# A transformer layer with attention and mixture of experts: the prologue rebuilt, in pairs of tiles

## The reference

```
h  = layernorm(x) * (1 + ca) + sa
xn = layernorm(h) * gamma + beta
q, k, v = xn @ qkv                       (256 wide each)
a  = softmax(q k^T / 16, causal) @ v @ o_proj + h
x  = x + ga * a
h2 = layernorm(x) * (1 + cb) + sb
gate: sigmoid(h2 @ gate_w^T), 2 of 4 groups, 4 of 32 experts, weights normalised, times 2
moe(h2): each expert takes at most 64 rows: silu(h2 w1) * (h2 w3) @ w2
shared(h2): silu(h2 sg) * (h2 su) @ sd
x  = x + gb * (moe(h2) + shared(h2))
```

## Time and profile before

| what | us |
|---|---|
| median of 3 runs | 187.12 (186.43 to 188.12) |
| span of the profiled execution (the page states no other time of its own for it) | 195.2 |
| TensorE busy | 155.4 (80%) |
| VectorE busy | 106.3 (54%) |
| ScalarE busy | 63.8 (33%) |
| GpSimd busy | 72.3 (37%) |
| first product of TensorE starts | 8.49 |
| product with vo for tile 3 ends | 60.5 |
| first scatter starts | 80.52 |

### The profile page before, as it was taken

How to read it: one execution, slowest core, us unless ns; L and a number is a source line. 1 busy time by engine, 2 the same in 40 slices (tenths; PEclk the granted TensorE clock), 3 DMA queues, 4 the chain that set the end, 5 groups by cost and what they waited for, 6 DMA issues and landing times.

```text
span 195.2 us, 2961 instructions
## 1 busy us (share of the span) xinstructions
PE 155.4 (80%) x1002; PEld 109.1 (56%) x1002; DVE 106.3 (54%) x377; ACT 63.8 (33%) x168; POOL 72.3 (37%) x96
## 2 busy tenths in 40 slices
PE   0298679999989999852992149995999969979984
PEld 0164437875558758631840034584877657569763
DVE  1589947459566979982142736792444523300453
ACT  3437876421457165330000125100264435400000
POOL 8129301995000000477776058540003726560000
PEclk9999999999999999999579556999699999999999
DMA  4999999999999900021100000009401101116992
GB/s 123 301 385 393 417 420 378 350 348 349 348 348 348 299 9 0 27 95 50 32 17 11 0 3 11 9 8 291 156 0 33 49 14 54 42 65 250 399 325 104
DMA packets 24670, 33.47 MB, mean 171 GB/s; under 512 B 2817, under 2 KB 19958, under 8 KB 24656
## 3 DMA queue, kind: packets, MB, share of 16 engines
q1 hardware_dynamic: 22352, 30.86, 46.1%
q0 software_dynamic: 2304, 2.44, 3.8%
HBM read 23.45 MB, written 13.83 MB: 191 GB/s over the span
## 4 chain that ended last, share of the span: by engine, by line
PE 30%; DVE 22%; DMA 12%; issue 11%; another core or an unknown queue 10%; ACT 6%; POOL 6%; SPq 1%; POOLq 1%; DVEq 0%; ACTq 0%
PE bank L997 7%; PE bank L1282 6%; DMA w_sb<-results 5%; POOL slots L437 4%; PE bank L1301 3%; DMA w_sb<-in_L_wmod_dram 3%; PE bank L1329 3%; PE bank L1261 3%; DVE bmax L768 2%; DMA arena<-slots 2%; DVE st L679 2%; POOL results L447 2%; DVE rows L789 2%; PE bank L1101 1%
## 5 line engine op out<-in xcount | busy, mean ns | idle before, releaser
L437 POOL DMA_INDIRECT slots<-rows,slot_idx x32 | 31.5, 984 | 52.0 <-DVE slot_idx L868 41.6
L447 POOL DMA_INDIRECT results<-arena,res_idx x16 | 15.6, 975 | 29.3 <-DVE arena L953 24.4
L1127 PE MATMUL bank<-arena 128*128 128x256 f32 x72 | 19.0, 411 | 0.4 <-issue 0.4
L1282 PE MATMUL bank<-w_sb,arena 128*64 128x128 f32 x256 | 17.7, 285 | 0.0
L1282 PEld LDWEIGHTS bank<-w_sb,arena 128*64 128x64 f32 x256 | 14.9, 143 | 2.4 <-issue 1.8
L1127 PEld LDWEIGHTS bank<-arena 128*128 128x128 f32 x72 | 14.3, 206 | 3.0 <-issue 0.9
L997 PE MATMUL bank<-w_sb,h2T 128*128 128x512 f32 x12 | 7.5, 760 | 8.5 <-DMA w_sb<-in_L_wmod_dram 8.5
L966 DVE TENSOR_TENSOR h2T<-h2T,bank 128x256 f32<-128x256 f32 x8 | 3.4, 422 | 15.5 <-ACT h2T L641 15.5
L539 ACT ACTIVATE h2T<-bank,modc 128x128 f32<-128x128 f32 x16 | 6.5, 455 | 14.1 <-PE bank L1135 12.5
L520 ACT ACTIVATE prob<-bank,nmax 128x512 f32<-128x512 f32 (+3 forms) x12 | 6.9, 581 | 12.4 <-DVE nmax L772 12.4
L1245 PE MATMUL bank<-ones_bf,ident_bf 128*128 128x128 bf16 x160 | 9.8, 219 | 1.1 <-issue 1.1
(11 more groups left out here) (155 smaller groups left out, 308.9 us busy)
## 6 DMA issues: line engine op xcount, KB each, us to landing
w_sb<-in_L_ffn_w_dram SPq DMA_DIRECT2D x12, 1024.0 KB, 12.4
results<-prob SPq DMA_DIRECT2D x1, 4096.0 KB, 22.0
w_sb<-results SPq DMA_DIRECT2D x7, 512.0 KB, 7.1
slots<-prob SPq DMA_DIRECT2D x1, 2112.0 KB, 12.1
arena<-slots SPq DMA_DIRECT2D x4, 528.0 KB, 5.5
xin<-in_L_attn_x_dram SPq DMA_DIRECT2D x4, 256.0 KB, 4.6
w_sb<-in_L_wmod_dram SPq DMA_DIRECT2D x1, 1024.0 KB, 9.7
out_dram<-base SPq DMA_DIRECT2D x8, 128.0 KB, 3.5
```

Source lines behind the costliest of these rows:

```text
L437: g.indirect_dma_start(out=slots_d, out_offset=bass.IndirectOffsetOnAxis(ap=slot_idx[:, i, k:k + 1], axis=0), in_=rows[:, i, :], in_offset ...
L447: g.indirect_dma_start(out=results_d, out_offset=bass.IndirectOffsetOnAxis(ap=res_idx[:, r:r + 1], axis=0), in_=ob[:, (r // 2) % 4, (r % 2 ...
L1127: last = t.matmul(bank[6][:, 0:H], probT[:, i % 2, j, :], vo[:, j, :], start=(j == 0), stop=(j == i))
L1282: last = t.matmul(bank[4 + g % 2][CAP * side:CAP * side + CAP, o:o + F], slotT[:, k, CAP * e:CAP * e + CAP], w[:, e, k, :], start=(k == 0) ...
```

## The change

It rebuilds what comes before tile 3.

- Loads: the modulation matrix comes in three loads instead of two, the first of them ahead of everything on SP's queue; x comes by pairs between the others; c is loaded from ScalarE's queue. `prob` is zeroed last of GpSimd's constants.
- TensorE first runs 56 products of a constant with itself (`keep_warm(WARM0)`), whose result nobody reads.
- h is made on VectorE alone, by pairs: (x - mean) * (1 + ca), then * rstd + sa, both in one instruction each per tile; ScalarE's `xhat_tile` and GpSimd's part are gone.
- q is made per pair in one bank and copied out by ScalarE; ScalarE also copies out v. The gate rows ga and gb are made one by one; GpSimd starts the residual rows after the first.
- The first tiles' scores, exps and products are mixed with the later pairs' h, q and v on every engine.

```
-            for j in range(NB):
+            def load_x(j):
                 sp.dma_start(xin[:, 2 * j:2 * j + 2, :], x_d[:, 2 * j:2 * j + 2, :]).then_inc(x_loaded[j], 16)
-                if j == 1:
-                    sp.dma_start(wmod_a, wmod_d[:, :, 0:512]).then_inc(wmod_loaded[0], 16)
+            sp.dma_start(wmod_a, wmod_d[:, :, 0:512]).then_inc(wmod_loaded[0], 16)
+            load_x(0)
             sp.dma_start(qkv_sb, qkv.rearrange("(p k) n -> p k n", k=KT)).then_inc(qkv_loaded, 16)
-            sp.dma_start(wmod_b, wmod_d[:, :, 512:1536]).then_inc(wmod_loaded[1], 16)
+            load_x(1)
+            sp.dma_start(wmod_b[:, :, 0:512], wmod_d[:, :, 512:1024]).then_inc(wmod_loaded[1], 16)
...
+            load_x(2)
+            load_x(3)
+            sp.dma_start(wmod_b[:, :, 512:1024], wmod_d[:, :, 1024:1536]).then_inc(wmod_loaded[2], 16)
...
-                    sp.wait_ge(qT_mm, 2)
+                    sp.wait_ge(qT_mm, NB)
...
-            pool.wait_ge(mod01, 1)
+            pool.wait_ge(gagb_done, 1)
             for i in range(NT):
-                if i % 4 == 0:
-                    continue
-                pool.wait_ge(xhat_done, i + 1)
-                g.tensor_tensor(h[:, i, :], h[:, i, :], mod[:, 1, :], ALU.mult).then_inc(xhat_scaled, 1)
-                if i % 2:
-                    pool.wait_ge(xhat_scaled, scaled_by_pool(i))
-                    g.tensor_tensor(h[:, i, :], h[:, i, :], mod[:, 0, :], ALU.add).then_inc(h_pool, 1)
...
+                pool.wait_ge(h_done, i + 1)
                 g.tensor_tensor(base[:, i, :], h[:, i, :], mod[:, 2, :], ALU.mult).then_inc(rbase_h, 1)
...
             def make_h(j):
...
+                for i in (2 * j, 2 * j + 1):
+                    step(v.scalar_tensor_tensor(out=h[:, i, :], in0=xin[:, i, :], scalar=mv1[:, i, 0:1],
+                                                in1=mod[:, 1, :], op0=ALU.subtract, op1=ALU.mult))
+                refine(X_STAT[j])
+                settle()
+                for i in (2 * j, 2 * j + 1):
+                    v.scalar_tensor_tensor(out=h[:, i, :], in0=h[:, i, :], scalar=rstd[:, 0, i:i + 1],
+                                           in1=mod[:, 0, :], op0=ALU.mult, op1=ALU.add).then_inc(h_done, 1)
+                dve.wait_ge(h_done, 2 * j + 2)
+                moments(H_STAT[j], h)
...
+            def keep_warm(count):
+
+                for _ in range(count):
+                    t.matmul(bank[0][:, 0:P], ones_bf[:, :], ones_bf[:, :], start=True, stop=True)
...
-                if j % 2:
+                if j == 1:
                     pe.wait_ge(modc_done, 1)
```

More of the change, by code:

```diff
@@ L307, in adaln_attention_moe @@
         MOD_BANK = [bank[b] for b in (0, 2, 7)]
+        Q_BANK = [bank[b] for b in (1, 3, 1, 3)]
+        VO_BANK = [bank[b] for b in (6, 7, 7, 7)]
         block = ctx.enter_context(nc.Block())
@@ L697, in refine @@
                                              in1=seed[:, which, r], op0=ALU.add, op1=ALU.mult))
-            def x_moments(n):
-                for j in (2 * n, 2 * n + 1):
-                    dve.wait_ge(x_loaded[j], 16)
-                moments(n, xin)
             def shift(n, done):
@@ L784, in add_attention @@
                 dve.wait_ge(x2_done, i + 1)
-                moments(6 + i, base)
+                moments(X2_STAT[i], base)
             def norm_x2(i):
-                refine(6 + i)
+                refine(X2_STAT[i])
                 v.tensor_scalar(rows[:, i, 0:H].rearrange("q (k p) -> q p k", k=KT),
@@ L1060, in turn_h, with project_q @@
                 last.then_inc(ring_filled, 1)
-            def project_q(half):
-                pe.wait_ge(ring_drained, ring[f"hn{2 * half + 1}"] + 1)
+            def project_q(j):
+                pe.wait_ge(ring_drained, ring[f"hn{j}"] + 1)
                 pe.wait_ge(wqk_done, 1)
-                if half:
-                    pe.wait_ge(qT_act, 1)
-                    pe.wait_ge(qT_dve, 1)
+                if j >= 2:
+                    pe.wait_ge(qT_done, j - 1)
                 for d in range(KT):
-                    last = product(bank[1 + 2 * d][:, :], [(wqk[:, k, P * d:P * d + P],
-                                                            xnT[:, k, 512 * half:512 * half + 512]) for k in range(KT)])
+                    last = product(Q_BANK[j][:, 256 * d:256 * d + 256],
+                                   [(wqk[:, k, P * d:P * d + P], xnT[:, k, 256 * j:256 * j + 256]) for k in range(KT)])
                 last.then_inc(qT_mm, 1)
@@ L1075, in project_v @@
                 pe.wait_ge(wvo_done, 1)
-                if j % 2:
+                if j == 1:
                     pe.wait_ge(modc_done, 1)
-                if j >= 2:
-                    pe.wait_ge(vo_done, j - 1)
+                elif j >= 2:
+                    pe.wait_ge(vo_done, j)
                 for i in range(2):
                     tok = slice(256 * j + P * i, 256 * j + P * i + P)
-                    last = product(bank[6 + j % 2][:, H * i:H * i + H], [(xnT[:, k, tok], wvo[:, k, :])
+                    last = product(VO_BANK[j][:, H * i:H * i + H], [(xnT[:, k, tok], wvo[:, k, :])
                                                                          for k in range(KT)])
@@ L1120, in weigh_v @@
                 if first == 0:
[L1121 removed]
+                    pe.wait_ge(vo_done, i // 2 + 1)
                     if i >= 1:
@@ L1240, in _ @@
                 last.then_inc(shd_mm, 1)
-            def keep_warm(count):
-                for _ in range(count):
-                    t.matmul(bank[0][:, 0:P], ident_bf[:, :], ones_bf[:, :], start=True, stop=True)
             pe.wait_ge(sh_hid, 4)
```

287 lines of the change are left out of this document (147 added, 140 removed).

## The result

| | before | after |
|---|---|---|
| median of 4 runs | 187.15 (186.43 to 188.12) | 201.19 (200.82 to 203.68) |
| ratio to before | | 1.075, 95% interval 1.068 to 1.081 |

I had forecast 193.4, with a range to 197.2. The direction was right, the size less than half: +6.3 against +14.0. The runs of the changed kernel lie at 200.8 to 201.3 and, once, at 203.7.

A forecast was written before the change was run, and what follows sets the result against it. TensorE's own work was taken to bound the prologue. Earlier start -1.7, less half-clock work -2.5 and idle rising from 4.35 to 14.9 gave +6.3 on the median 187.1: 193.4 us, range 188.5 to 197.2.

The forecast's parts named there:

- The clock falls in a wait: Rival: long TensorE waits drop its clock to half speed, each fall costing up to 3.4 us; 196.8 us, chance 0.14.
- the line of the ledger that carried TensorE's work over at full speed: TensorE's prologue: real work stays the same, 0 us change apart from 2.5 us less half-clock work at the start.
- second and fourth waits: TensorE idle before turning hn pair 1, 4.35 us, and before turning hn pair 3, 4.7 us.
- the walk: Step through the engines' lists up to tile 3's product, adding TensorE's idle to 14.9 us and the shift to +6.3.
- Part of it taken up by the next wait: In the clock rival: each fall costs TensorE up to 3.4 us, partly absorbed by the following wait.
- the two signs that I had named for being wrong: TensorE idle under 8.5 us in the first 60 us, or VectorE idle stretches from 37 to 50 us.
- The other sign: TensorE's idle in the first 60 us being under 8.5 us would show the forecast wrong.
- The idle: TensorE's waits up to tile 3's product: 0.3 + 2.4 + 4.35 + 1.6 + 0.45 + 1.05 + 4.7 = 14.9 us, against 4.35 before.
- third wait: TensorE idle of 1.6 us before turning hn pair 2; the zeroing's delay of the exps hidden by 0.4.
- The start: TensorE's first real product at 6.8 us after warming, 1.7 us earlier than 8.49.
- The 4.2 us that I counted as gain: Start of TensorE's list: 1.7 us from the earlier start and 2.5 us from no half-clock work.
- Behind the prologue: After tile 3's product no order changes; its shift moves the first scatter and the end by as much.

The follow-up runs named there:

- experiment 1: Changed kernel with products of a constant with itself filling four TensorE waits; ratio to before 1.030 in its first run, 1.041 again.
- second filled run: Repeat of the changed kernel with four TensorE waits filled by products of a constant with itself; 195.97 us for 187.34, ratio 1.041.
- experiments 5 and 6: Changed kernel, one move each: hn pair 3 turned behind score 4, ratio 1.038; hn pair 1's shift directly behind make_h(1), 204.6 us against 196.0, unclear as timed.
- experiment 3: Changed kernel run again unedited, 200.36 us, ratio 1.061; and without its 56 warming products at the start, 203.38 us, ratio 1.076.
- experiment 4: Kernel before with the first modulation load in front, c on ScalarE's queue, 56 warming products and later zeroing; 196.18 us against 195.98, ratio 1.004.
- two moves: Changed kernel with hn pair 1's shift directly behind make_h(1) and hn pair 3 turned behind score 4; 189.80 us, ratio 1.003.
- The second profile of before: Kernel before, unedited, profiled again on the chip that shows holes behind the first scatter; 195.72 us, span 193.6.
- the repeat: Changed kernel run again without any edit; 200.36 us against 188.36, ratio 1.061.

## Why the prediction was wrong

**The step that failed** is the rival "The clock falls in a wait", and with it the line of the ledger that carried TensorE's work over at full speed. I had seen a fall before, priced it at up to 3.4 us, and wrote that my second and fourth waits were longer than that one. Then I gave it 0.14, counted it once, and left it out of the forecast. At its own price two falls would have given 187.1 + 6.3 + 6.8 = 200.2. In the trace there are three falls, 7.8 us, and filling four waits took 6.3 to 6.8 us back (experiment 1). That 6.3 + 7.8 is the measured shift to 0.1 is partly chance, for not all of the 7.8 was on the path: with the waits filled the shift is still 7.4 to 7.9, so by this measure the walk itself was 1.1 to 1.6 short. The Trainium skill, page "TensorE: Matmul & The Clock Gate", section "HAM oscillation — how this bites in real kernels", describes it as something paid again at each wait that comes round, not once; the trace agrees, with three stretches at three waits, though the waits of 2.02 and 1.70 us had none. It was also not bound to long waits: the one of 1.89 us was followed by the longest stretch, 38.8 to 45.6.

**"Part of it taken up by the next wait"** was true of little. The slow value product at 42.66 did not hide in a wait, it made one: ScalarE copies v before it gives the seed for the last x pair, and VectorE stood 2.71 us for it (VectorE, changed kernel):

```profile
47.16 0.16 DVE L696 TENSOR_TENSOR newt<-half_v,seed 128x2 f32<-128x2 f32 x1 [2.71 <-ACT seed L463]
```

In the second filled run 1.27 of this wait is left, so a little over half is the clock's. What is slow on TensorE is late on VectorE two engines on. This was one of the two signs that I had named for being wrong: idle of VectorE between 37 and 50 us, where I had it at work (2.71 here, and 2.79 before attention 0 at 40.60). The other sign, less than 8.5 us of idle, did not come. The product ended at 74.62, outside the 64 to 69 that I had written.

**The idle** was walked well as far as the sum goes. Forecast and measured, in order: 2.4 and 2.02; 4.35 and 5.51; 1.6 and 1.89; 0.45 and none; 1.05 and 1.70; 4.7 and 4.02; loads and small 0.3 and 0.88. Sum 14.9 and 16.0 (16.08 with small gaps). The terms miss by up to 1.2 and partly cancel. In the third wait the walk's own numbers hide the zeroing by 0.25 (33.35 against 33.1), not by the 0.4 it states. The two long waits were where I put them, with the releaser I named, and experiments 5 and 6 removed each by moving what I had named as standing ahead.

**The start** was 0.9 earlier than forecast. In a ledger with a start and an idle term this is no error, since the idle grows by what the start gains. What it is worth by itself is not shown: without the warming the list of the changed kernel is 1.3 to 1.5 us late until the clock hides it (0.4 at tile 3's product, experiment 3), and the edit to the kernel before gave 0.0 because, by VectorE's rows, it put x behind the modulation load (experiment 4). The 4.2 us that I counted as gain arrived in neither.

**Behind the prologue**: the shift is passed on, 14.2 at the first scatter and 13.6 in the span.

## What to carry to other kernels

When a list of TensorE's gets new waits, price each wait twice: its length, and the work behind it at half speed, and follow the slow work to the engines that read it. Before redesigning, move what needs nothing into the wait: two moves, of one call on VectorE and one on TensorE with ScalarE's copies in step, gave back 11.3 to 11.6 of 14 us here. An earlier start is worth only what the next wait does not swallow, and when a load is moved forward, look at what now stands behind it. A difference of 1 us in one profile can be the clock's: compare the granted clock of both before giving it to the edit.

## What the hardware showed that I had not expected

- One chip of those used ran every kernel with holes behind the first scatter: the kernel before took 195.98 there (median of 13 runs), and 188.36 and 187.34 on two others (19 and 17). The engines stand for 2.5 to 3.6 us with no releaser on their own core ("remote", "issue"):

```profile
90.87 0.42 DVE L860 TENSOR_TENSOR xin<-xin,bank 128x256 f32<-128x256 f32 x1 [3.53 <-remote]
91.44 1.05 PE L997 MATMUL bank<-gateT,h2T 128*128 128x32 f32 x8 [2.55 <-issue]
```

  (The second profile of before, VectorE and TensorE.) Their cause stays open.
- Whether the clock falls at a wait is not a matter of its length alone. In the changed kernel's first profile 2.02 us before turn 0 did not, 1.89 before turn 2 did; in the repeat 2.21 us there was followed by a turning at 0.66 and the fall came behind it.
- The same kernel's ratio to before was 1.075 and 1.061 in two sessions, with intervals that barely touch: an interval covers one session on one chip.
